# An LSTM recommender on one core: row gathers paced by ScalarE's activations instead of TensorE's tiles, tile counts of the seven-product cells raised at once, and some ELU, copy and embedding steps moved

## The reference, cut to what matters

```python
rp = concat([region_tbl[region_idx], poi_tbl[poi_idx]])          # rows of 8 and 4
nv = concat([rp @ W_rp + b_rp, coords @ W_co + b_co])
conv = elu(conv1d(nv, conv_w, 'VALID') + conv_b)                 # 10 -> 8 steps, 32 wide
emb = tanh(concat([car_tbl[car_idx], week_tbl[week_idx], time_tbl[time_idx]]))
x = concat([conv, broadcast(emb)])
h = lstm(x, Wih0, Whh0, ...)      # g = x@Wih.T + h@Whh.T + b; i, f, g, o
h = lstm(h, Wih1, Whh1, ...)      # c = s(f)*c + s(i)*tanh(g); h = s(o)*tanh(c)
return ((h[:, -1] @ W1 + b1) @ W2 + b2) @ W3 + b3
```

## Time and profile before

| what | value |
|---|---|
| time, median of 3 runs | 1069.15 us (1068.37 to 2749.66) |
| the profiled execution's own time | 1068.24 us, of which the span is 1066.4 us |
| TensorE busy | 1027.5 us (96%) |
| VectorE, ScalarE, GpSimd busy | 810.0, 668.1, 351.0 us |
| granted TensorE clock, mean | 0.991 |
| gathers (L740) | 160 region, 120 poi, 16 car, 16 time; median 947 ns each |

### The profile page before, as it was taken

One profiled execution on the slowest core, in us unless ns is written; L12 is line 12 of the kernel. 1 busy time (PEld: TensorE's weight loads), 2 busy tenths in 40 slices (PEclk: granted clock), 3 DMA queues, 4 the chain that ended last, 5 costly groups with the idle time before them and its releaser, 6 DMA issues.

```text
span 1066.4 us, 15685 instructions
## 1 busy us (share of the span) xinstructions
PE 1027.5 (96%) x6129; PEld 627.9 (59%) x6129; DVE 810.0 (76%) x1135; ACT 668.1 (63%) x1029; POOL 351.0 (33%) x353
## 2 busy tenths in 40 slices
PE   8699999999999999999999999999999999999997
PEld 6444444477445666676545567766644577666645
DVE  5489889976768878677787886777686887878654
ACT  2466444577565767777664676767755577777743
POOL 7660066645430046553540025663631000000000
PEclk9799999999999999999999999999999999999999
DMA  9310100000111010000010110000010100000001
GB/s 258 80 18 14 30 3 2 3 2 2 14 21 40 2 33 2 3 2 2 2 32 1 40 32 3 3 3 2 3 31 2 40 22 10 1 1 2 1 1 40
DMA packets 32092, 21.43 MB, mean 20 GB/s; under 512 B 19629, under 2 KB 25865, under 8 KB 32019
## 3 DMA queue, kind: packets, MB, share of 16 engines
q1 hardware_dynamic: 21223, 19.25, 6.3%
q0 software_dynamic: 9984, 1.12, 2.7%
q10 hardware_dynamic: 812, 0.07, 0.1%
HBM read 9.92 MB, written 4.19 MB: 13 GB/s over the span
## 4 chain that ended last, share of the span: by engine, by line
PE 80%; DVE 11%; issue 4%; ACT 4%; another core or an unknown queue 0%; DVEq 0%; POOL 0%; ACTq 0%; POOLq 0%
PE acc L1967 29%; PE acc L2001 13%; PE aux L2001 13%; PE acc L1958 12%; PE acc L1952 4%; DVE gates L1379 2%; PE aux L2282 2%; PE acc L1779 2%; ACT gates L938 1%; DVE h_part L1581 1%; DVE t_part L1546 1%; DVE h_full L1574 1%; PE acc L2107 1%; PE acc L2116 1%; PE aux L1867 1%
## 5 line engine op out<-in xcount | busy, mean ns | idle before, releaser
L1967 PE MATMUL acc<-h_part,wh 128*128 128x512 f16 x1824 | 445.9, 380 | 0.0
L1967 PEld LDWEIGHTS acc<-h_part,wh 128*128 128x128 f16 x1824 | 160.4, 98 | 217.6 <-issue 53.5
L740 POOL DMA_INDIRECT feat<-in_L_rec_region_tbl,region_idx x160 | 173.6, 1085 | 148.8 <-PE aux L2001 45.8
L1379 DVE TENSOR_TENSOR gates<-acc,emb_gates 128x512 f32<-128x512 f32 x239 | 157.1, 682 | 22.8 <-PE acc L1967 16.1
L938 ACT ACTIVATE gates<-gates,gate_bias,unscale 128x512 f32<-128x512 f32 x168 | 128.3, 806 | 65.0 <-DVE gates L1379 62.8
L740 POOL DMA_INDIRECT feat<-in_L_rec_poi_tbl,poi_idx x120 | 132.4, 1103 | 93.5 <-PE acc L1967 33.9
L1958 PE MATMUL acc<-h_part,wh 128*128 128x512 f16 x624 | 148.6, 379 | 0.3
L1952 PE MATMUL acc<-x_in,wx 96*128 96x512 f32 x239 | 132.8, 562 | 0.8 <-DVE gates L1379 0.8
L923 ACT ACTIVATE gates<-acc,gate_bias,unscale 128x512 f32<-128x512 f32 x110 | 81.8, 780 | 77.1 <-PE acc L1967 54.0
L1958 PEld LDWEIGHTS acc<-h_part,wh 128*128 128x128 f16 x624 | 59.8, 98 | 75.5 <-issue 4.4
L2001 PE MATMUL aux<-t_part,w_form 128*128 128x256 f16 x816 | 94.8, 273 | 0.0
(11 more groups left out here) (239 smaller groups left out, 1451.7 us busy)
## 6 DMA issues: line engine op xcount, KB each, us to landing
out<-y SPq DMA_DIRECT2D x16, 256.0 KB, 2.1
x_in<-conv_hi SPq DMA_DIRECT2D x56, 64.0 KB
feat<-in_L_rec_region_tbl,region_idx POOLq DMA_INDIRECT x160
w<-in_L_rec_W SPq DMA_DIRECT2D x4, 512.0 KB, 5.2
w_nat<-in_L_rec_Whh SPq DMA_DIRECT2D x2, 1024.0 KB, 8.3
w<-in_L_rec_W SPq DMA_DIRECT2D x1, 2048.0 KB
feat<-in_L_rec_poi_tbl,poi_idx POOLq DMA_INDIRECT x120
x_in<-conv_lo SPq DMA_DIRECT2D x28, 64.0 KB
```

The costliest lines, as they stand in the source:

```text
L740: pool.indirect_dma_start(out, None, tables[k], bass.IndirectOffsetOnAxis(ap=rows, axis=0)).then_inc(landed, DMA)
L1379: nc.vector.tensor_tensor(gates[0][:, j, g, :], source, emb_gates[:, g * HK + j, :], ALU.add).then_inc(gate_sum, 1)
L1967: mm = nc.tensor.matmul(bank, wh[:, own_w, a, c, rows], h_part[layer][:, s.read_slot, b, c, :], start=False, stop=(c == HK - 1 and a == LO))
```

## The change: what it does, and the diff

Six edits. (1) In `wait_tile`, POOL waits for `gate_act` (raised by ScalarE's activation of a tile) where it waited for `gate_acc` (raised by TensorE at the tile's end). (2) The 56 gathers are spread over 60 tiles, (1,1) to the fourth of (0,6), where it was 48 tiles, (0,3) to (1,4); the 32 later ones over 44 tiles where they were one to each of 30. (3) In the seven-product cells TensorE raises `gate_acc[1]` by 8 in the last product; it was seven increments, spread over the cell. (4) At t = 5 ACT makes its two copies to B1 and B2 first, then the copy of the turned features, then four quarters, then the two tanhs of the embeddings; all three extra steps stood ahead of the first copy. (5) DVE's `split_emb` moves behind `both_c`. (6) ELU pieces 3 to 8 move: four steps later in the upper cell, so that three of the `part_sums` come ahead of pieces 5 to 8.

```diff
-                            pool.wait_ge(gate_acc[at[0]], at[1])
+                            pool.wait_ge(gate_act[at[0]], at[1])
...
-                    begun = list(pace(n, [(0, 3), (1, 2), (0, 4), (1, 3), (0, 5), (1, 4)]))
+                    begun = list(pace(n, [(1, 1), (0, 3), (1, 2), (0, 4), (1, 3), (0, 5), (1, 4), (0, 6)]))[:-4]
...
-                    tiles = pace(n, [(1, 5), (0, 7), (1, 6), (0, 8)])
+                    begun = list(pace(n, [(1, 5), (0, 7), (1, 6), (0, 8), (1, 7), (0, 9)]))[:-2]
+                    rows = GR * 2 * (T - WIN)
+                    tiles = (begun[i * len(begun) // rows] for i in range(rows))
...
                     nc.scalar.copy(bank, source).then_inc(part_copy, 1)
+                if s.feeds is not None:
+                    put_turned(feat_t[:, 0, :], aux[0:KF, 0, :], turned[0], s.feeds + 1, turned_put[0])
                 for bank, pair, step in ((B1, (GATE_I, GATE_G), 3), (B2, (GATE_F, GATE_O), 4)):
                     act.wait_ge(part_acc, steps + step)
                     for a, g in enumerate(pair):
                         quarter(s, 0, g, LEFT, half_bank(bank, a))
+                if s.feeds is not None:
+                    emb_tanhs(s.feeds, aux[:, 2, :])
...
-                x_piece(4)
+                x_piece(3)
                 both_ig(low)
                 both_fc(low)
                 both_c(low)
-                x_piece(5)
-                x_piece(6)
+                if s.feeds is not None:
+                    split_emb(s.feeds)
+                x_piece(4)
                 both_h(low)
...
-                x_piece(7)
                 part_sums(s, 0)
                 if low.forms is not None:
                     t_low(low)
+                part_sums(s, 1)
+                part_sums(s, 2)
+                x_piece(5)
+                x_piece(6)
+                part_sums(s, 3)
+                x_piece(7)
+                both_ig(s)
                 x_piece(8)
-                for k in range(1, ADDS7):
-                    part_sums(s, k)
-                both_ig(s)
...
-                product(A1, FIRST_PAIR, A11, B11, True, 1)
+                product(A1, FIRST_PAIR, A11, B11, True)
...
-                product(E2, SECOND_PAIR, S4, B22, False, 2)
+                product(E2, SECOND_PAIR, S4, B22, False)
                 pe.wait_ge(part_sum, sums + 3)
-                product(A2, SECOND_PAIR, A22, T4, False)
+                product(A2, SECOND_PAIR, A22, T4, False, 8)
```

More of the change, by code:

```diff
@@ L74, in __init__ @@
         self.opens7 = False
+        self.feeds = None
         self.early = False
@@ L220, in body @@
         end = fast(last_t - 2)
+        end.feeds = n + 1 if following else None
         yield "upper", end, low[1]
@@ L1102, in _ @@
                     n, c = stage[1:]
-                    put_turned(feat_t[:, c, :], aux[0:KF, c, :], turned[c], n + 1, turned_put[c])
-                elif kind == "turn_emb":
-                    emb_tanhs(stage[1], aux[:, 2, :])
+                    if c == 1:
+                        put_turned(feat_t[:, 1, :], aux[0:KF, 1, :], turned[1], n + 1, turned_put[1])
                 elif kind == "emb_gates":
@@ L1611, in lower @@
                         add_embeddings(s, *place)
-                        if s.makes_x:
+                        if s.makes_x and k < 3:
                             elu_piece(chunk_of(s.batch, 1), s.batch, k)
@@ L1747, in _ @@
                 kind = stage[0]
-                if kind == "turn_emb":
-                    split_emb(stage[1])
-                elif kind == "conv":
+                if kind == "conv":
                     n, c = stage[1:]
@@ L2023, in fast_cell @@
                     pe.wait_ge(gate_act[1], s.tile)
-                product(A1, FIRST_PAIR, A11, B11, True, 1)
+                product(A1, FIRST_PAIR, A11, B11, True)
                 product(A2, SECOND_PAIR, A11, B11, True)
                 pe.wait_ge(part_copy, copies + 1)
-                product(B1, FIRST_PAIR, A12, B21, False, 1)
+                product(B1, FIRST_PAIR, A12, B21, False)
                 pe.wait_ge(part_copy, copies + 2)
@@ L2033, in fast_cell @@
                 pe.wait_ge(forms_ready, 2 * FORMS)
-                product(E1, FIRST_PAIR, S1, T1, True, 1)
+                product(E1, FIRST_PAIR, S1, T1, True)
                 product(A1, FIRST_PAIR, S2, T2, False)
                 pe.wait_ge(gate_sum, low.tile + 8)
-                product(E2, SECOND_PAIR, S1, T1, True, 1)
+                product(E2, SECOND_PAIR, S1, T1, True)
                 pe.wait_ge(part_copy, copies + 3)
                 product(E1, FIRST_PAIR, S4, B22, False)
-                product(A2, SECOND_PAIR, S2, T2, False, 1)
+                product(A2, SECOND_PAIR, S2, T2, False)
                 pe.wait_ge(part_copy, copies + 4)
@@ L2043, in fast_cell @@
                 pe.wait_ge(part_copy, copies + 6)
-                product(A2, SECOND_PAIR, S3, T3, False, 1)
+                product(A2, SECOND_PAIR, S3, T3, False)
                 pe.wait_ge(part_sum, sums + 2)
```

## The result

The changed kernel took 1081.57 us (median of 4 runs, 1077.31 to 1082.05) against 1068.76 for the kernel before, of which one run took 2749.66 us and another 1059.46. The ratio, of fast runs alone, is 1.015, with a 95% interval of 1.0117 to 1.0183. It is slower, by less than 2%. The forecast, 1061.5 us, lies on the other side of no change, and its range ended at 1072. The profiled execution has a span of 1079.6 us, 13.2 more than before, at a mean granted clock of 0.986 (before 0.991).

A forecast was written before the change was run, and what follows sets the result against it. TensorE, busy 96% of the span, bounds the kernel; only its idle stretches can be won. Terms -1.7 - 1.2 + 0 - 4.7 = -7.6 on 1068.24, plus 0.9 for the median: 1061.5 us, range 1053 to 1072.

The forecast's parts named there:

- The mechanism: Upper cells beside gathers: a long unbroken run holds back TensorE's increments, whichever semaphore POOL waits for; 12.75 us in excess.
- the price of (1) and (2): Seven-product and lower cells: the new pace wins 12.7 us of holds and costs 8, net -4.7 us.
- The break ahead of the upper cell: Pause in gathers before an upper cell, at best 1.3 us; where it fails, 7 cells lose 0.3 us each: +2.
- The hand-over: Lower cells, where the run of 11 gathers moves: 12 hand-overs at 0.5 us each, +6 us.
- Rival A: Lower cells: each of 12 hand-overs loses 1.5 us, 1071.5 us in all; at 2.3 us each 1081; chance 0.25.
- The turn: Turn of t = 5: the last gather's rows land before TensorE needs them, slack 0.2 to 0.8 us, cost 0.
- rival C: Turn of t = 5, three batches: TensorE waits up to 2 us for gathers, +6, 1067.5 us; chance 0.07.
- (4) with (5): Cells of t = 5: copies to B1 start in time, embeddings split while DVE waits; 3 x 0.57, -1.7 us.
- (6): Cells with ELU pieces: the 0.76 us wait goes, 0.37 returns at the next copy to B1; three times, -1.2 us.
- (3): Seven-product cells: merging TensorE's increments changes nothing, 0 us; the Trainium skill's page would give an estimated 2.7 us less.
- Rival B: Upper cells: all holds go, perhaps through fewer TensorE increments or ScalarE's pace breaking the runs; 1053.5 us, chance 0.15.

The follow-up runs named there:

- one_burst: Kernel before, with all 56 gathers of each of three batches waiting only for the first tile of (0,3): ratio 1.0001 on a prompt chip, 1.1629 (1238.7 us) late.
- best2: Changed kernel with one gather per TensorE tile from (0,3), spread increments restored, ELU pieces shifted once more: ratio 0.9926 on a prompt chip, 0.9843 (1048.5 us) late.
- act_late_start: Changed kernel with the gathers of batch 1 begun at (0,3), not (1,1): 1047.11 us, ratio 1.0004, on a prompt chip.
- early_rows: Changed kernel with the 56 gathers spread over 56 tiles, (1,1) to (1,4), none waiting for (0,6): 1043.82 us, ratio 0.9969, on a prompt chip.
- only_456: Kernel before with edits (4), (5) and (6) alone; pace, lists and increments as before: 1043.96 us, ratio 0.9970, on a prompt chip.
- no_step3: Changed kernel with edit (3) undone, the seven increments of the products put back: 1046.33 us, ratio 0.9992, on a prompt chip.

## Why the prediction was wrong

**The mechanism was right, its reach was not.** That a long unbroken run of gathers holds back TensorE's increments is what one_burst and best2 show on the late chip. That which semaphore POOL waits for does not matter by itself is borne out in part: the runs of the changed kernel, released by ScalarE, and that of one_burst, released by TensorE, both hold; ScalarE's pace without long runs was not tried on a late chip. Shown too: all of the holding is bound to a chip or its condition, which no row of the profile before could tell.

**The step that failed is the price of (1) and (2)**, -12.7 + 8 = -4.7 in the prediction. Measured, it is +16.4: the whole 13.2, and the 3.2 that edits (4) to (6) won. Of these, 9.7 fell up to 182 us in batch 0, 4.1 in the upper cells of t = 2 to 4 and 2.6 in the cells with the turns. Its parts:

- *The break ahead of the upper cell, "7 with 0.3 us: +2".* The prediction put the break at 1.3 us at best and none at worst, and priced it as if even then the run would be young. It was none: the run of 11 was one of 14 and 15, across the head of the upper cells of t = 2 and 3, the place without slack. These cells and those of t = 4 lie 5.65, 2.37, 0.42, 6.67, 2.55 and 0.43 us above 18.48, 18.1 in sum, of which 2 x 0.6 belong to edit (6). It was to be 2 and was 16.9, more than the 12.75 of before. The sum took the hold as a matter of where the run lies, though by its own reading it is the end of a long run that holds: the run has to be counted from its first gather.
- *The hand-over, +6.* It cost nothing; lower cells without a turn stay at 12.4 to 12.5 us. Rival A at its worst, 1081, met the total by luck, through a place where nothing happened.
- *Batch 0, not priced at all.* The prediction took its gains from the seven-product cells and asked only there what the new list does. But the list now begins at (1,1), and POOL cannot begin before DVE has the poi indices. Eight waits for tiles already past (the last of them by 132 us) make eight gathers in a row, and the run goes on to 14: +9.1 us between 146 and 182 us, the largest single item. That the run there does it is by the timeline; the version without it (act_late_start) met only prompt chips, so no pair of runs shows it. best2 with a run of 8 at that place on the late chip lost nothing.
- *The turn, 0 with a slack of 0.2 to 0.8 us.* It was rival C, at 0.5 to 0.7 us of waiting for each batch, 1.9 us in all; the cells grew by 2.6. On a prompt chip early_rows takes it away.

**The small steps held.** (4) with (5): forecast -1.7, measured -2.4; the cell of t = 5 is clean. (6): forecast -1.2; its three cells gained 2.6 and, by batch 3, gave back 0.6 each behind them (forecast 0.37), so -0.8. only_456 against one_burst, both on prompt chips, shows the same 0.9 and 0.6 in each of the three batches. (3): forecast 0, and no_step3 shows no difference, on a prompt chip alone. Together with (4) and (5), (6) gave 3.0 us in only_456, forecast 2.9. Rival B's thought that fewer increments might loosen the holds was not tried by itself on a late chip; with them the changed kernel's holds were no shorter.

On a prompt chip, in short, the forecast's small terms are nearly all there is: -3.0 of moved steps, and 1.4 to 2.0 lost at the turns.

## What to carry to other kernels

A list that says which event releases each of a row of transfers must be read at its start too: events that are past when the issuer first gets there release everything at once. Where indirect gathers are issued beside a full TensorE, keep unbroken runs to six or eight, one gather to an event that comes more slowly than a gather takes (1.25 us here): it costs nothing on a chip that does not mind, and was worth some 10 us on one that does (an estimate, from 17.3 us there less the 7.3 that the same kernel wins on a prompt chip). A short break may not be enough: in the kernel before, two runs of 6 with 1.3 us between them (381.1 to 397.9 us) stand beside the cell of t = 2 that took 20.43 us in place of 18.48. And before small edits are weighed, run the kernel on more than one chip: a profile can hold a loss that belongs to its chip.

## What the hardware showed that was not expected

- Chips differ. The kernel before took 1046.5 to 1047.1 us in five sets and 1065.8 and 1068.8 in two, with TensorE's increments late in the latter alone. What sets such a chip, or its condition, apart stays open; POOL's gathers are no longer there (busy 53 to 55 us for 56, against 56 to 61).
- The recording may have a part in it. Every timed run here has a span and a granted clock of its own, so as far as the record tells each was recorded. On the late chips the recorded semaphore events have gaps up to the last gather and none behind it. The same thing that holds TensorE may make the recording lose events, or the recording may be what holds it; no run here tells these apart, nor what a late chip does when nothing is recorded.
- On such a chip, late in a run of 56 gathers, TensorE starts an instruction only every 1.4 us, and ScalarE stood up to 32 us for one of its increments. ScalarE's own increments are not late in the cells.
- In idle stretches of 3.8 to 4.0 us (2.56 us in the kernel before, ahead of 645.86) or right behind them TensorE's granted clock fell to its lower level, 1.2 GHz, for 3.4 to 6.8 us: 0.93 and 0.86 on the mean of the two t = 2 cells, 0.92 before the change, and 0.61 in the run of 56 where TensorE stood for 52 of 70 us.
